# A gated cross-attention and Sinkhorn-mixing kernel: the squares ahead of v's copy, one tile of x behind the softmax inverse, and GpSimd paced by VectorE

## The reference, cut to what matters

```python
def attention(qk, v):              # 16 patches of 128 columns per batch, 8 heads of 32 rows
    q, k, val = Wq @ qk + bq, Wk @ qk + bk, Wv @ v + bv
    attn = softmax(q.T @ k / sqrt(32), axis=-1)     # 128 x 128 for each head
    return (Wo @ gelu(attn @ val) + bo) * masks

def mixing(x):                     # each row of 2048 is 4 streams of 512
    xn = x * rsqrt(mean(x * x) + eps)
    H_res = sinkhorn(xn @ W_res.T + base, iterations=50)   # a 4 x 4 matrix for each row
    H_pre, H_post = softmax(xn @ W_pre.T + ..), softmax(xn @ W_post.T + ..)
    y = (sum over streams of H_pre * x) @ W_branch
    return H_res mixed streams + H_post * y

x = x + tanh(g0) * attention(layernorm(x), ctx)
x = x + tanh(g1) * mixing(layernorm(x))
```

## Time and profile before

| | |
|---|---|
| Time, 3 runs | median 1775.77 us (1771.59 to 1778.42) |
| The profiled execution | 1780.68 us, of which the span is 1778.9 us |
| Busy: PE, PE weight loads, DVE, ACT, POOL | 79%, 50%, 72%, 64%, 45% of the span |
| Mean granted TensorE clock | 0.924 of full speed |

### The profile page before, as it was taken

How to read it: one execution, slowest core, us unless ns; L and a number is a source line. 1 busy time by engine, 2 the same in 40 slices (tenths; PEclk the granted TensorE clock), 3 DMA queues, 4 the chain that set the end, 5 groups by cost and what they waited for, 6 DMA issues and landing times.

```text
span 1778.9 us, 36533 instructions
## 1 busy us (share of the span) xinstructions
PE 1412.3 (79%) x12644; PEld 890.2 (50%) x12800; DVE 1288.7 (72%) x3526; ACT 1143.7 (64%) x2337; POOL 807.7 (45%) x1373
## 2 busy tenths in 40 slices
PE   1769999988888988888888889888888897427735
PEld 0446566555554555554555455555555565224424
DVE  3334434566678888888788888887787778767988
ACT  2457877777677777776677667777677766423312
POOL 3323335355645563656555564556455644440000
PEclk9889999999999999998999999999999998768878
DMA  8557776666666767676677757676566544422123
GB/s 247 155 150 206 186 192 182 184 173 173 186 176 198 204 176 198 198 196 190 166 206 199 203 153 206 196 192 168 171 171 180 145 120 128 107 83 95 71 71 142
DMA packets 175464, 299.95 MB, mean 169 GB/s; under 512 B 25104, under 2 KB 76176, under 8 KB 171184
## 3 DMA queue, kind: packets, MB, share of 16 engines
q1 hardware_dynamic: 157872, 264.04, 49.5%
q0 software_dynamic: 17408, 33.56, 11.0%
HBM read 179.81 MB, written 67.11 MB: 139 GB/s over the span
## 4 chain that ended last, share of the span: by engine, by line
DVE 30%; PE 25%; ACT 14%; POOL 13%; issue 13%; SPq 3%; DMA 2%; DVEq 0%; POOLq 0%; ACTq 0%
PE pr L693 8%; PE pr L707 7%; POOL kp L583 7%; DVE ssum L1326 5%; ACT squares L998 3%; DVE sv L1327 3%; DVE xpre L1343 2%; POOL x1c L518 2%; DVE otile_even L1355 2%; DVE otile_even L1372 2%; DVE x1c L1222 2%; DVE sa L1327 2%; DVE negm L1204 2%; DVE otile_odd L1355 2%; ACT g_sb L976 2%
## 5 line engine op out<-in xcount | busy, mean ns | idle before, releaser
L583 POOL TENSOR_TENSOR kp<-ke,sv 128x64 f32<-128x64 f32 x329 | 149.3, 454 | 281.6 <-DVE sv L1327 280.9
L1326 DVE TENSOR_REDUCE ssum<-kp 128x16 f32<-128x64 f32 x768 | 182.2, 237 | 124.7 <-POOL kp L583 117.9
L499 POOL TENSOR_TENSOR x_hl<-xc,x_hl 128x512 bf16<-128x512 f32 x128 | 156.4, 1222 | 153.2 <-ACT x_hl L926 153.1
L707 PE MATMUL pr<-wv,ctx_hl 128*128 128x256 bf16 x1536 | 199.7, 292 | 29.4 <-DVE k_hl L1189 22.6
L583 POOL TENSOR_TENSOR kp<-ke,sa 128x64 f32<-128x64 f32 x343 | 149.7, 436 | 143.1 <-DVE sa L1327 143.0
L1212 DVE TENSOR_TENSOR o_sb<-av_ps,rden 128x128 f32<-128x128 f32 x256 | 72.7, 284 | 192.7 <-ACT rden L967 189.2
L1204 DVE TENSOR_REDUCE negm<-s_ps 128x4 bf16<-128x512 f32 x256 | 166.7, 651 | 61.3 <-PE s_ps L813 60.9
L840 PE MATMUL av_ps<-probs,v_t 128*32 128x128 f32 x2048 | 112.0, 289 | 124.0 <-DVE o_sb L1212 123.7
L693 PE MATMUL pr<-x_hl,wq 128*128 128x512 bf16 x707 | 171.5, 387 | 43.2 <-POOL x_hl L499 36.5
L693 PE MATMUL pr<-x_hl,wk 128*128 128x512 bf16 x736 | 195.3, 421 | 5.9 <-issue 4.5
L958 ACT ACTIVATE probs<-st_ps,key_bias 128x512 f32<-128x512 f32 x256 | 173.6, 678 | 36.9 <-PE st_ps L827 36.6
(11 more groups left out here) (171 smaller groups left out, 3096.4 us busy)
## 6 DMA issues: line engine op xcount, KB each, us to landing
xs<-in_dram SPq DMA_DIRECT2D x128, 256.0 KB, 5.7
xc<-in_dram SPq DMA_DIRECT2D x128, 256.0 KB, 4.3
ctx_raw<-in_dram SPq DMA_DIRECT2D x32, 1024.0 KB, 7.4
x1c<-in_dram POOLq DMA_DIRECT2D x64, 512.0 KB, 7.5
x_dram<-x1c SPq DMA_DIRECT2D x32, 1024.0 KB, 5.2
q_st<-q_hl SPq DMA_DIRECT2D x384, 64.0 KB
k_st<-k_hl SPq DMA_DIRECT2D x384, 64.0 KB
x1t_even<-x_dram SPq DMA_DIRECT2D x16, 1024.0 KB, 5.9
```

The lines of the kernel that those rows point to most:

```text
L499: nc.gpsimd.tensor_tensor(x_hl[:, G % 2, 1, t, :], xc[:, t, :], x_hl[:, G % 2, 0, t, :], ALU.subtract).then_inc(x_split, 1)
L583: nc.gpsimd.tensor_tensor(kp[:], ke[:], v, ALU.mult).then_inc(kp_made, 1)
L707: ins = nc.tensor.matmul(bank(what)[:, j * E:(j + 1) * E], ctx_hl[:, a, t, win], wv[:, m, t, :], start=(t == 0 and a + m == 0), stop=(t == ...
L1326: cf.link(nc.vector.tensor_reduce(s_t, k, AX.X, ALU.add))
```

## The change

Three edits. In unit 4, `banked_at` lists v's projection behind the two transposes instead of ahead of them, and ACT makes the three squares ahead of the copy of v. In unit 5, ACT normalizes and rounds its tile of x behind the inverse of the softmax sum, instead of ahead of the exponential. In units without an iteration, from the third batch on (`2 * UNITS <= g < NU`), POOL waits at two places of its body: for the maximum of g, and for the division of g-2.

```diff
--- before.py
+++ after.py
@@ -140,10 +140,12 @@
     assert len(made) < 2
     if 0 <= G + 1 < NG:
         made += {0: [("q", G + 1, 0)], 1: [("q", G + 1, 1)], 2: [("k", G + 1, 0)], 3: [("k", G + 1, 1)],
-                 4: [("v", G + 1, 0)], 7: [("v", G + 1, 1)]}.get(r, [])
+                 7: [("v", G + 1, 1)]}.get(r, [])
     if 0 <= G - 1 < NG and r in (5, 6):
         made += [("o", G - 1, 2 * (r - 5)), ("o", G - 1, 2 * (r - 5) + 1)]
     made += [("t", H, j) for H, j in at_step(g, 2, T_AT)]
+    if r == 4 and 0 <= G + 1 < NG:
+        made.append(("v", G + 1, 0))
     made += [("lg", H, 0) for H, j in at_step(g, 2, [LOGITS_AT])]
     made += [("pre", f, t) for f, t in tiles_at(g, "pre")]
     if g == -2:
@@ -616,6 +618,10 @@
                 for ready in ffn_at(g, COEF_AT):
                     coefficients(ready)
 
+                paced = its == (None, None) and 2 * UNITS <= g < NU
+                if paced:
+                    pool.wait_ge(max_done, g + 1)
+
                 low = at_step(g, -1, LOW_CTX_AT)
                 for H, t in low[:1]:
                     split_ctx(H, t)
@@ -634,6 +640,8 @@
                 for ready in ffn_at(g, STAT_AT + 2):
                     scale_b(ready, 0)
                 scale_at(f, its, 2)
+                if paced:
+                    pool.wait_ge(o_done, g - 1)
                 for H, t in low[1:]:
                     split_ctx(H, t)
                 if 0 <= G - 1 < NG and r == 4:
@@ -1110,13 +1118,18 @@
 
                 for H, t in at_step(g, -1, HI_CTX_AT):
                     hi_ctx(H, t)
-                for H, t in at_step(g, -2, HI_X_AT):
+                x_now = at_step(g, -2, HI_X_AT)
+                for H, t in x_now if r != 5 else []:
                     norm_x(H, t)
                     hi_x(H, t)
                 if 0 <= g - 1 < NU:
                     exp_scores(g - 1)
                 if 0 <= g - 2 < NU:
                     inverse_den(g - 2)
+
+                for H, t in x_now if r == 5 else []:
+                    norm_x(H, t)
+                    hi_x(H, t)
                 for done, t in tiles_at(g, "first"):
                     first_products(done, t)
                 for done, t in tiles_at(g, "diag"):
@@ -1137,7 +1150,12 @@
                     for ready in ffn_at(g, RETURN_AT + n):
                         answer(ready, 5 + n)
                 made = banked_at(g)
+                squared = at_step(g, 2, SQUARES_AT)
                 for n, what in enumerate(made):
+                    if what[0] == "v" and r == 4:
+                        for H, t in squared:
+                            square_x1(H, t)
+                        squared = []
                     if what[0] in "qk":
                         read_qk(what)
                     elif what[0] == "v":
@@ -1148,7 +1166,7 @@
                         copy_lg(what)
                     elif what[0] in ("pre", "mix"):
                         copy_pre(what)
-                for H, t in at_step(g, 2, SQUARES_AT):
+                for H, t in squared:
                     square_x1(H, t)
                 if g == FIRST + UPC + 3:
                     w_parts(2, wv, wv_loaded)
```

## The result

The changed kernel took 1714.92 us (median of 4 runs, 1709.18 to 1715.88) where the kernel before took 1773.68 us beside it: a ratio of 0.9672, 95% interval 0.9651 to 0.9693. The prediction was 1715 us. The profiled executions are 71.5 us apart (1780.68 and 1709.18), 10 more than the 61 of the sum. I call the way from chunk 10's first row maxima on DVE to chunk 31's the late stage. It took 1011.47 us before and takes 947.76 us now.

The account below looks back on a forecast made before the run. PE bounds the stage without iterations; late, PE and DVE wait for one another through ACT. 40.0 + 4 - 1.5 + 14.5 + 4 = 61 us off 1780.7 gives 1719.7, less 4.9 for the median: 1715 us, range 1692 to 1757.

Parts of the forecast that it names:

- the 61 of the sum: Whole kernel: 40.0 + 4 - 1.5 + 14.5 + 4 = 61 us less, from 1780.7 to 1719.7 us for a profiled execution.
- Edits 1 and 2, 40 us, with 4 for chunks 7 to 9: ACT, units 4 and 5: earlier inverse shortens DVE's unit 5 waits, 40.0 us in chunks 10 to 30, 4 in 7 to 9.
- the wait of 0.94 us for v goes: ACT, unit 4 of chunk 20: squares need only x1, so this wait goes; with the x tile's 1.37, 2.31 us.
- My caps: Unit 5, chunks 10 to 30: gains limited by DVE's 2.19 us wait, PE's waits (near 1.75) and ACT's 2.31.
- Chunks 2 to 6 lose 1.5 us: Unit 4 where PE is full: second transposes, now ahead of v, wait for `k_hl`'s bank; 5 x 0.3 us lost.
- Edit 3, 14.5 us: Late stage's logits' softmax: with POOL paced, six batches fall from 22.44 us to 1.2 each; 14.5 of 15.2 taken.
- The clock, 4 us, bounds 0 and 14: PE's k projection behind unit 2's wait: a shorter wait could save ten chunks up to 1.4 us each; 4 taken.
- Half of it arrives: Rival, chance 0.20: DVE, running ahead, meets another wait (`f`, `s_ps` or POOL's `kp`), 0.3 to 1 us each; 1745 us.
- Slower: Rival, chance 0.05: paced POOL tiles collide with DVE's stream additions, up to 76 us, 15 above the gain; 1791 us.
- Division of unit 5 without a wait: Expected profile sign on DVE: the division in unit 5 has no wait, or one under 0.5 us.
- PE's wait of unit 1 gone: Expected profile sign on PE: its wait for DVE's division in unit 1, 1.12 us in chunk 21, disappears.
- That of unit 2 near 1.2: Expected profile sign on PE: its wait for DVE's division in unit 2 shrinks from 1.90 to about 1.2 us.

## Why the prediction was right, and where it was off

The number was right; the sum that led to it had errors of both signs.

- **Edits 1 and 2, 40 us, with 4 for chunks 7 to 9.** Right in place and mechanism: DVE's wait for the inverse in unit 5 of chunk 20 is gone, ScalarE is ahead, the squares' sums reach GpSimd earlier. Too small: the two edits gave 54.3 and 58.1 us. The step that failed is "the wait of 0.94 us for v goes", taken from chunk 20 for all. It averages 2.3 us (47.6 over 21), and 3.7 and 3.2 in classes 1 and 3. By class, the sum had 10.5 us for class 0, 8.8 for class 1, 12.6 for class 2 and 8.1 for class 3; the two profiles of edits 1 and 2 show 14.2 and 15.7, 16.8 and 16.5, 6.9 and 4.9, 13.0 and 12.8. So three classes were sized too small, and that of the softmax at about twice what came. In chunk 22 of the first of them DVE's wait did fall from 3.93 to 1.66 us, but PE's 4.33 us behind the softmax stayed. Classes 1 and 3 gave more than DVE had stood in unit 5 there (2.84 us a chunk in class 1; 2.19 or 0.89 in class 3), and how is not shown step by step. My caps were read from one state of the chain, and PE's unit 4 in class 1 had a clock of 0.77 before and 0.92 after. Chunks 7 to 9 gave 3.6.
- **Edit 2 beside edit 1.** I added 0.94 and 1.37 us as if both counted in full. With the squares ahead alone, DVE's wait in unit 5 was already down from 42.8 to 17.3 us, and what was left stood mostly in class 2. So edit 2, worth 19.4 alone, added 12 on top.
- **Chunks 2 to 6 lose 1.5 us.** Chunks 2, 3 and 4 went from 36.90 to 37.21 us each, the 0.3 sized, but the stretch as a whole from 191.1 to 190.6, and to 193.0 in the second profile of the full change: a loss of 1.5 us is not told apart there.
- **Edit 3, 14.5 us.** Too large as a share: 9.4 on top of the others, though 19.3 alone. The softmax itself came out as sized, 22.44 to 6.84 us for 7 forecast, PE's wait 1.48 for 1.5. Part of what PE gains there it then waits in unit 4 (1.11 us for `k_hl`; 0.41 before). By the Trainium skill (SBUF — State Buffer, section Who interferes with whom), a DVE instruction with two SBUF inputs contends with a GpSimd instruction that reads SBUF, and the lock is exclusive. The batch took 1.12 us with GpSimd waiting and 3.98 us with it free to run, which agrees. The gain that the same rule would promise for DVE's other instructions appeared as busy time (818.12 to 812.77 us) and not as time.
- **The clock, 4 us, bounds 0 and 14.** Probably the term that was sized worst. PE's busy time fell by 23.4 us in the late stage. At the half that the dummy products showed, some 12 us of the result are the clock's (7 to 14 by the interval). That is an estimate from another kernel's ratio, not shown for this one.
- **The rivals.** "Half of it arrives" did not happen, although its sign is there: PE's new wait of 1.94 us in unit 3, and DVE's in unit 6. "Slower" by collisions: DVE's busy time fell, and of the 64 stream additions in units 17 to 23 of the batches in the late stage two lasted 1.10 us, the others 0.75 us at most. PE never waited for `low_gelu`: its first output product of unit 5 in chunk 22 has 0.16 us ahead of it, as before.
- **What the profile would show.** Division of unit 5 without a wait: right in classes 0, 1 and 3 (chunk 28's 0.5 us apart), wrong in class 2, with 0.9 to 1.8 us, and 5.0 in chunk 10. PE's wait of unit 1 gone: right in chunk 21, still 0.8 to 1.1 us in chunks 12, 16 and 20. That of unit 2 near 1.2: 1.2 to 1.7 in most chunks, 1.8 to 1.9 in four, with one of 1.94 behind it in unit 3 in most, which I had not foreseen.

So the forecast of 1715 was met by errors of both signs. With its 4 us for the clock the sum gave the two ScalarE edits 46.5 us and the pacing 14.5. Timed beside one another they are 58.1 and 9.4 us, 67.5 together; the first timing of the full change had 58.8, and the 61 of the sum lies between the two. That the number itself was met to 0.1 us is luck in good part: the two timings of the gain are 8.7 us apart, and I took the profiled run of before to lie 4.9 us above its median, while that of after lay 5.7 us below its own.

## What to carry to other kernels

A wait that repeats in a loop is not sized from one pass: add it up by class over all passes before multiplying, since one slow engine (here PE, behind a longer wait and at its lower clock) can triple it in half of them. When an engine waits for data that comes in the same stage each time, put its independent work ahead of the wait; here three moved squares were worth 2.6%. Once one edit has taken the wait that a second one aims at, the second is worth what is left, and removing a wait further on may be worth nothing, so edits in one chain are not added.

## What was not expected of the hardware

- Doing more on PE saved time: 222 dummy products in its waits took the time at 1.2 GHz in the late stage from 98.8 to 27.2 us and the kernel from 1779.11 to 1761.63 us. The waits ahead of which they stood were mostly 1.9 us long, and unit 2 of chunk 21, behind one, had a granted clock of 0.78.
- In part the low clock moves rather than ends. Units 2, 3 and 4 had 34.1, 30.7 and 34.1 us of it in the late stage before, and 6.8, 20.5 and 23.9 after the change. In class 3 unit 2 went from 0.87 to 0.95 on average, while unit 3 fell from 1.00 to 0.89.
- The waits alone do not decide it. In the kernel with the squares alone ahead, PE waited 1.75, 1.95 and 1.85 us in units 2 to 4 of chunk 21, and the granted clock was 1.00 in all three. What decides it no run here shows.
- A lower clock on PE shows up as a wait on ScalarE: v took 4.29 us in chunk 21 instead of 2.79 in chunk 20, which is 1.50 of the 2.59 us by which the copy waited longer (3.53 against 0.94).
